# Causal attention scores from three bf16 parts of q and k, prepared by GpSimd and DMA

## What is computed

```python
q, k, v = (proj(Wq), proj(Wk), proj(Wv))
q = q * cos + _rotate_half(q) * sin      # the same for k
scores = jnp.einsum('bhqd,bhkd->bhqk', q, k) / math.sqrt(d)
scores = scores + causal
tmp_sum = jnp.sum(softmax(scores), axis=-2)
_, topk_idx = jax.lax.top_k(tmp_sum, heavy_budget)   # 25 of 256 keys per head
mask = heavy_mask | band                 # |i - j| <= 25
scores = jnp.where(mask, scores, neg)
attn = softmax(scores) @ v
x = x + attn @ Wo.T
```

## Time and profile before

| | |
|---|---|
| median of 3 runs | 2241.49 us (2239.89 to 2243.34) |
| the profiled execution | 2239.64 us, its span 2237.8 us |
| TensorE matmul busy | 2033.8 us |
| VectorE, ScalarE, GpSimd busy | 1325.7, 950.0, 230.7 us |
| granted TensorE clock, mean | 0.947 of full |

### The profile page before, as it was taken

How to read it: one execution, slowest core, us unless ns; L and a number is a source line. 1 busy time by engine, 2 the same in 40 slices (tenths; PEclk the granted TensorE clock), 3 DMA queues, 4 the chain that set the end, 5 groups by cost and what they waited for, 6 DMA issues and landing times.

```text
span 2237.8 us, 86088 instructions
## 1 busy us (share of the span) xinstructions
PE 2033.8 (91%) x34733; PEld 1748.2 (78%) x34733; DVE 1325.7 (59%) x4942; ACT 950.0 (42%) x3354; POOL 230.7 (10%) x346
## 2 busy tenths in 40 slices
PE   5889999999996889766999999998999989999999
PEld 3677677767665768666898998898998988988987
DVE  3565575575565079555666666665666656666653
ACT  1355364464453212233444444443444444444432
POOL 0011011011102100000011010110110110111012
PEclk9999999999997999865899999999999999999999
DMA  6000000000000832200000000000000000000000
GB/s 249 1 1 0 0 0 0 0 0 0 0 1 32 291 113 73 67 17 3 18 17 18 13 18 18 27 4 19 27 4 28 18 19 13 18 18 13 4 12 10
DMA packets 53629, 66.07 MB, mean 30 GB/s; under 512 B 4384, under 2 KB 45792, under 8 KB 52416
## 3 DMA queue, kind: packets, MB, share of 16 engines
q1 hardware_dynamic: 50832, 46.48, 6.2%
q0 software_dynamic: 2448, 14.68, 2.0%
HBM read 44.34 MB, written 16.81 MB: 27 GB/s over the span
## 4 chain that ended last, share of the span: by engine, by line
PE 51%; DVE 4%; issue 2%; ACT 1%; DMA 0%; DVEq 0%; POOL 0%; ACTq 0%
PE ps L1302 27%; PE ps L1256 11%; PE ps L1236 11%; PE ps L1290 2%; PE ps L1245 1%; DVE hbuf L1472 1%; DVE dh L1460 0%; DVE dh L1466 0%; DVE hbuf L1469 0%; DVE cn L1450 0%; DVE ns L1462 0%; DVE h L1470 0%; ACT nn L1369 0%; DVE s L1438 0%; DVE cn L1438 0%
## 5 line engine op out<-in xcount | busy, mean ns | idle before, releaser
L1302 PE MATMUL ps<-hbuf,whf 128*128 128x32 f16 x24480 | 659.1, 178 | 82.9 <-DVE hbuf L1472 59.9
L1302 PEld LDWEIGHTS ps<-hbuf,whf 128*128 128x128 f16 x24480 | 648.3, 97 | 106.0 <-DVE hbuf L1472 60.4
L1349 ACT ACTIVATE rz<-s,sc 128x32 f32<-128x32 f32 x512 | 164.5, 321 | 524.1 <-DVE s L1438 512.6
L1236 PE MATMUL ps<-hbuf,w1f 128*128 128x256 f16 x2304 | 294.4, 275 | 0.0
L1256 PE MATMUL ps<-hh,w2f 128*128 128x256 f16 x2304 | 294.1, 276 | 0.0
L1438 DVE TENSOR_REDUCE s<-ps 128x32 f32<-128x64 f32 x512 | 114.5, 224 | 272.7 <-PE ps L1302 259.4
L1425 POOL TENSOR_TENSOR hh<-tb,hh 128x256 f16<-128x256 f32 x192 | 132.3, 694 | 1307.2 <-ACT hh L1396 1307.2
L1236 PEld LDWEIGHTS ps<-hbuf,w1f 128*128 128x128 f16 x2304 | 224.5, 98 | 33.3 <-issue 6.0
L1256 PEld LDWEIGHTS ps<-hh,w2f 128*128 128x128 f16 x2304 | 212.0, 98 | 45.9 <-issue 19.6
L946 PE MATMUL ps<-x1T,wi 128*128 x768 | 173.7, 389 | 21.2 <-DMA wi<-in_W_ih 12.6
L946 PEld LDWEIGHTS ps<-x1T,wi 128*128 128x128 f32 x768 | 149.1, 195 | 45.4 <-issue 19.6
(11 more groups left out here) (198 smaller groups left out, 2876.3 us busy)
## 6 DMA issues: line engine op xcount, KB each, us to landing
gi_d<-stage SPq DMA_DIRECT2D x96, 128.0 KB, 1.7
gi<-gi_d SPq DMA_DIRECT2D x16, 768.0 KB, 5.5
w1f<-in_w1T POOLq DMA_DIRECT2D x4, 1408.0 KB, 9.2
xall<-in_x SPq DMA_DIRECT2D x4, 1024.0 KB, 9.0
x1T<-in_xT SPq DMA_DIRECT2D x1, 4096.0 KB, 21.7
w2f<-in_w2T POOLq DMA_DIRECT2D x2, 2048.0 KB, 11.0
out<-x1T SPq DMA_DIRECT2D x8, 512.0 KB, 3.1
wi<-in_W_ih SPq DMA_DIRECT2D x1, 3072.0 KB, 10.5
```

The source lines that it names most:

```text
L1236: last = nc.tensor.matmul(ps[:, 6 + i % 2, 0:TT], w[:, wp, e % EH, c * P:(c + 1) * P], hbuf[par][:, k, hq, :, :].rearrange("p s b -> p (s ...
L1302: last = nc.tensor.matmul(ps[:, bank, g * WIDE * 2 * B:(g + 1) * WIDE * 2 * B], whp[:, k, w, q, g * P:(g + 1) * P], h[:, k, :, :].unsqueez ...
L1349: nc.scalar.activation(rz[:, q, :, :].rearrange("p g b -> p (g b)"), s1[:, q, :, :].rearrange("p g b -> p (g b)"), ACT.Sigmoid, scale=sc[: ...
```

## The change

- TensorE no longer makes the rotation partner. SP copies the swapped halves of each 32 channels from `raw` to a tile `swp`, in 8 DMAs of 16 partitions for q and 8 for k.
- VectorE rotates in `raw` itself, in three operations each for q and k, and these stand one by one inside the second pass of the batch before, behind the work of heads 1, 2, 3, 5, 6 and 7 (`ROTATE_AT`).
- GpSimd splits the rotated float32 tile into three bf16 parts of falling size whose sum is the value (`split`: cast, subtract, cast, subtract). The four steps for q and the four for k stand ahead of the diagonals of heads 4 to 11 (`SPLIT_AT`).
- SP stores the six parts to DRAM and reads them back into `pk`, where the 32 channels of a head lie three times over on 96 partitions, each time another part (`SLOTS`). Two such stacks (`way`) hold six of the nine products of parts. A quarter of `pk` is one channel tile: 12 DMAs of 32 x 4 rows of 512 bytes. Quarter m is filled once the second pass of the batch before has done its heads.
- A score is now four bf16 products over 96 partitions: two of 128 columns, two of 256. The first pass waits at heads 0, 4, 8 and 12 for the quarters. `rot`, `kz`, `tmp` and their operations are gone.

```diff
-        rot = sb(st, "rot", [P, 2, KD, S])
-        kz = sb(st, "kz", [P, HPC, KD, S])
+        swp = sb(st, "swp", [P, KD, S])
+        parts = sb(st, "parts", [P, 2, 3, KD, S], BF16)
+        pk = sb(st, "pk", [3 * DH2, 2, 2, HPC, KD, S], BF16)
+        parts_d = nc.dram_tensor("parts_d", [2, 3, P, KD * S], BF16).ap()
...
+            @block.sync
+            def _(sp):
+                def swap(b, i):
+                    sp.wait_ge(a_raw, b * 2 + i + 1)
+                    half = DH2 // 2
+                    for to in range(0, P, half):
+                        of = to + half if to % DH2 == 0 else to - half
+                        sp.dma_start(swp[to:to + half, :, :], raw[of:of + half, i, :, :]).then_inc(d_swap, 16)
+                def store_parts(b, i):
+                    sp.wait_ge(g_part, (b * 2 + i + 1) * 4)
+                    for j in range(3):
+                        sp.dma_start(parts_d[i, j], parts[:, i, j, :, :].rearrange("p m s -> p (m s)"))\
+                            .then_inc(d_parts, 16)
+                def pack(m):
+                    for i in range(2):
+                        for way in range(2):
+                            for slot, j in enumerate(SLOTS[i][way]):
+                                of = parts_d[i, j].rearrange("(q d) n -> d q n", d=DH2)
+                                sp.dma_start(pk[slot * DH2:(slot + 1) * DH2, i, way, :, m, :],
+                                             of[:, :, m * S:(m + 1) * S]).then_inc(d_pack[m], 16)
+                def prepare(b, first):
+                    if not first:
+                        sp.wait_ge(v_rot, b * 6)
+                    swap(b, 0)
+                    sp.wait_ge(v_rot, b * 6 + 3)
+                    swap(b, 1)
+                    if not first:
+                        for m in range(KD):
+                            sp.wait_ge(d_pack[m], b * PACK)
+                    for i in range(2):
+                        store_parts(b, i)
+                    sp.wait_ge(d_parts, (b + 1) * 6 * 16)
+                    for m in range(KD):
+                        if not first:
+                            sp.wait_ge(p_s, b * 2 * NH - NH + (m + 1) * HPC + 1)
+                        pack(m)
+                for b in range(B):
+                    prepare(b, b == 0)
...
+                def split(b, i, step):
+                    if step == 0:
+                        pool.wait_ge(v_rot, b * 6 + 3 * i + 3)
+                        if b:
+                            pool.wait_ge(d_parts, b * 6 * 16)
+                    else:
+                        pool.wait_ge(g_part, (b * 2 + i) * 4 + step)
+                    x = raw[:, i, :, :]
+                    part = [parts[:, i, j, :, :] for j in range(3)]
+                    if step == 0:
+                        last = nc.gpsimd.tensor_copy(part[0], x)
+                    if step == 1:
+                        last = nc.gpsimd.tensor_tensor(x, x, part[0], ALU.subtract)
+                    if step == 2:
+                        last = nc.gpsimd.tensor_copy(part[1], x)
+                    if step == 3:
+                        last = nc.gpsimd.tensor_tensor(part[2], x, part[1], ALU.subtract)
+                    last.then_inc(g_part, 1)
+                def diagonals(b, more):
                     pool.wait_ge(v_l, b + 1)
                     for h in range(NH):
+                        if more and h in SPLIT_AT:
+                            j = SPLIT_AT.index(h)
+                            split(b + 1, j // 4, j % 4)
...
+                def batch(b, more):
                     pool.wait_ge(p_v, b + 1)
                     nc.gpsimd.tensor_copy(hb[:, :, :], hT[:, :, bass.ds(b, 1), :].rearrange("p k a s -> p k (a s)"))\
                         .then_inc(c_hb, 1)
-                    diagonals(b)
+                    diagonals(b, more)
+                for j in range(8):
+                    split(0, j // 4, j % 4)
+                for b in range(B):
+                    batch(b, b < B - 1)
...
-                    if r == 0 and h == 0:
-                        pe.wait_ge(v_rot, b * 6 + 6)
-                    if r == 0 and h < 2:
-                        pe.wait_ge(a_kz, b * 2 + h + 2)
-                    elif r == 0 and h < HPC:
-                        pe.wait_ge(v_kz, b * 2 + h - 1)
+                    if r == 0 and h % HPC == 0:
+                        pe.wait_ge(d_pack[h // HPC], (b + 1) * PACK)
...
-                    nc.tensor.matmul(ps[:, bank, 0:P], rot[:, 0, m, 0:P], kz[:, q, m, 0:P],
-                                     start=False, stop=True, skip_group_check=True)
-                    nc.tensor.matmul(ps[:, bank, P:P + S], rot[:, 0, m, P:S], kz[:, q, m, :],
-                                     start=False, stop=True, skip_group_check=True).then_inc(p_s, 1)
+                    for way in range(2):
+                        nc.tensor.matmul(ps[:, bank, 0:P], pk[:, 0, way, q, m, 0:P], pk[:, 1, way, q, m, 0:P],
+                                         start=False, stop=(way == 1), skip_group_check=True)
+                    for way in range(2):
+                        last = nc.tensor.matmul(ps[:, bank, P:P + S], pk[:, 0, way, q, m, P:S],
+                                                pk[:, 1, way, q, m, :],
+                                                start=False, stop=(way == 1), skip_group_check=True)
+                    last.then_inc(p_s, 1)
...
-                def swap(b, i):
-                    pe.wait_ge(a_raw, b * 2 + i + 1)
-                    for m in range(KD):
-                        last = nc.tensor.matmul(ps[:, 4 + 2 * i + m // 2, (m % 2) * S:(m % 2 + 1) * S],
-                                                tab[:, C_ROT:C_ROT + P], raw[:, i, m, :],
-                                                start=(m % 2 == 0), stop=True, skip_group_check=True)
-                    last.then_inc(p_rot, 1)
...
-                    if more:
-                        swap(b + 1, 0)
                     pe.wait_ge(a_o, (b + 1) * KD)
-                    if more:
-                        swap(b + 1, 1)
...
+                        if late:
+                            act.wait_ge(g_part, b * 8)
...
-                    act.wait_ge(v_rot, b * 6 + 6)
-                    for q in range(2):
-                        nc.scalar.activation(kz[:, q, :, :].rearrange("p m s -> p (m s)"),
-                                             rot[:, 1, :, :].rearrange("p m s -> p (m s)"), ACT.Copy,
-                                             scale=tab[:, C_HEAD + q:C_HEAD + q + 1]).then_inc(a_kz, 1)
...
-                def rotate(b):
-                    for i, (c, s) in enumerate(((C_COSQ, C_SINQ), (C_COSK, C_SINK))):
-                        dve.wait_ge(p_rot, b * 2 + i + 1)
-                        if i == 0:
-                            dve.wait_ge(p_s, b * 2 * NH + 1)
-                            dve.wait_ge(a_kz, b * 2 + 1)
-                        cos = tab[:, c:c + S].unsqueeze(1).broadcast_to((P, KD, S))
-                        sin = tab[:, s:s + S].unsqueeze(1).broadcast_to((P, KD, S))
-                        nc.vector.tensor_tensor(tmp[:, :, :],
-                                                ps[:, 4 + 2 * i:6 + 2 * i, :].rearrange("p a (m s) -> p (a m) s", s=S),
-                                                sin, ALU.mult).then_inc(v_rot, 1)
-                        nc.vector.tensor_tensor(rot[:, i, :, :], raw[:, i, :, :], cos, ALU.mult).then_inc(v_rot, 1)
+                def rotate(b, i, step):
+                    c, sn = ((C_COSQ, C_SINQ), (C_COSK, C_SINK))[i]
+                    cos = tab[:, c:c + S].unsqueeze(1).broadcast_to((P, KD, S))
+                    sin = tab[:, sn:sn + S].unsqueeze(1).broadcast_to((P, KD, S))
+                    if step == 0:
+                        dve.wait_ge(d_swap, (b * 2 + i + 1) * 8 * 16)
+                        nc.vector.tensor_tensor(swp[:, :, :], swp[:, :, :], sin, ALU.mult).then_inc(v_rot, 1)
+                    if step == 1:
+                        nc.vector.tensor_tensor(raw[:, i, :, :], raw[:, i, :, :], cos, ALU.mult).then_inc(v_rot, 1)
+                    if step == 2:
                         dve.wait_ge(v_rot, b * 6 + 3 * i + 2)
-                        nc.vector.tensor_tensor(rot[:, i, :, :], rot[:, i, :, :], tmp[:, :, :], ALU.add)\
+                        nc.vector.tensor_tensor(raw[:, i, :, :], raw[:, i, :, :], swp[:, :, :], ALU.add)\
                             .then_inc(v_rot, 1)
-                        dve.wait_ge(v_rot, b * 6 + 3 * i + 3)
-                    for q in range(2, HPC):
-                        nc.vector.tensor_scalar(kz[:, q, :, :], rot[:, 1, :, :], tab[:, C_HEAD + q:C_HEAD + q + 1],
-                                                None, ALU.mult).then_inc(v_kz, 1)
...
-                    if more:
-                        rotate(b + 1)
+                        if more and h in ROTATE_AT:
+                            j = ROTATE_AT.index(h)
```

(25 more changed lines are left out.)

11 lines of the change are left out of this document (3 added, 8 removed).

## The result

The changed kernel takes **2347.6 us** (median of 4 runs, 2336.8 to 2353.5) against 2242.1 (4 runs, 2239.9 to 2243.3): 1.047 times as long, 95% interval 1.042 to 1.051. The profiled execution took 2343.6 us, its span is 2341.7. The time lies inside the range on record, but 46 us above the predicted 2302 and 2 us under the range's upper end of 2350; two of the four runs are above that end. The change cost 105 us where 62 were forecast.

A forecast was written before the change was run, and what follows sets the result against it. Three engines stand together near the first pass's bound; GpSimd's splits would hold up the second. Seven longer periods +32, contention +14, clock +10, start +16, last batch -10: +62 on 2239.6 gives 2302 us, range 2262 to 2350.

The forecast's parts named there:

- First pass: First score to end of the `lcol` copy: ScalarE sets the pace at 0.95 us per head, 36.0 instead of 38.6.
- Contention: Second pass: `En` delayed by shared access with GpSimd, 2 us per batch between bounds 0 and 6, +14 in all.
- the chain on record: Second pass: rotations, GpSimd's splits, diagonals and maxima step by step, last `En` at 39.7 us after `lcol` instead of 26.0.
- Tail: Last `En` to the next batch's first score: 10.4 us instead of 15.4, the wait for rotation and `kz` gone.
- Clock: TensorE's lower granted clock, charged to second pass and before the output product: 1.5 us per batch (0 to 3.5), +10.
- Last batch: Both passes without rotation or split: first gains 4.6 us, second takes 22.7 instead of 28.2; -10.
- Start: Batch 0, swaps, rotation, split and packs without cover: first quarter packed at 89.6 against 74.4; +16 us.
- The third rival: Second attention: contention and clock at their upper bounds, period 95.6 us, 2351 us in all; chance 0.20.

The follow-up runs named there:

- Small splits: Changed kernel with the four split operations covering 32 elements instead of 1024 from batch 1 on, at their places: 2301.4 us.
- late ones: Changed kernel with the eight split steps before the diagonals of heads 8 to 15 instead of 4 to 11: 2317.4 us.
- the scores alone: Kernel before the change, with scores as bf16 products of the new shape on a constant tile, rotation and `kz` as before: 2213.2 us.
- the run with more TensorE work: Changed kernel with eight extra mask products, result overwritten, before the second-pass scores of heads 4 to 11: 2342.2 us.
- one way: Changed kernel with each score multiplying only the first of its two packed stacks, 384 columns instead of 768: 2362.8 us.
- adds first: Kernel before the change, with VectorE's two `kz` operations behind its four `x1T` adds instead of ahead of them: 2224.1 us.

## Why the prediction was right, and where it was short

*Right: direction, bound, place.* GpSimd's split, in one queue with the diagonals, sets the second pass: TensorE waits 105.2 us for them. Small splits (-46) and late ones (-30) confirm it. They also show how near the next bound stands: with the waits for diagonals at 2.8 us, VectorE's own chain still took 39.7. The subtract is 2.12 us (taken as 2.2 between 1.04 and 2.8). The single steps of the chain held while nothing contended: q rotated 9.7 (10.1), maxima of head 4 12.6 (12.6), of head 5 15.2 (15.4). TensorE waited for packs in batch 0 only. The gain of the scores was small because three engines stand together at the first pass's bound, as the scores alone show.

*First pass: 37.1, not 36.0.* ScalarE kept its pace (14 heads in 13.5 us, 0.96 each), but value products started 14.4 us after the first score, not 13.2: a set of light-sum products (L581) stood ahead of score 15, waited 0.66 us for VectorE and took 0.86, which my count left out.

*Contention: the term that failed.* I took 2 us per batch of bounds 0 and 6, arguing that VectorE has slack where GpSimd is the bound. It has none behind a blocked `En`. Against the chain on record, k was rotated at 24.5 instead of 22.7, 1.8 of it from the `En` pair at 433.70; head 11's maxima began at 34.9 instead of 32.5, another pair behind the second subtract of k; and heads 12 to 15 took 1.8 more again, 1.2 of it one pair behind a diagonal and the copy of `hb`, the rest a pitch of 1.28, not 1.19 us. That pitch is no contention: the scores-only run has it too. In VectorE's rows of the changed kernel's batch 3:

```profile
448.50 1.71 DVE L795 TENSOR_SCALAR En<-E,rl 128x128 f32<-128x128 f32 x1
450.13 0.72 DVE L797 TENSOR_SCALAR En<-E,rl 128x256 f32<-128x256 f32 x1
...
453.35 0.71 DVE L795 TENSOR_SCALAR En<-E,rl 128x128 f32<-128x128 f32 x1
453.98 1.12 DVE L797 TENSOR_SCALAR En<-E,rl 128x256 f32<-128x256 f32 x1
```

Against an undisturbed pair (0.55 us from the start of the one to the end of the other) the three lose 1.8, 1.8 and 1.2 us, not all of it on the chain (the pairs of heads 4 and 8 lose 1.2 each as well, beside the second casts); the pass came out at 43.9 in this batch and 44.3 on the mean, against 39.7 + 2. So contention cost some 4 us per batch, 25 to 30 us in all instead of +14, and well towards the bound of 6, though by another pair of instructions: the `En` operations, not the rotation products (their mean of 1.22 is unchanged here, since GpSimd had no split to do beside them). Only with splits later did a rotation product meet one.

*Tail: 11.6, not 10.4*, with a gap of 0.89 us before the next batch (under 1 was forecast). It goes with the clock: the tail took 10.7 us in the three batches that had 1.00, and 12.0 to 12.4 in the four that had 0.86.

*Clock.* Of the 1.5 charged per batch the tail shows 0.9 (11.6 on the mean for 10.7 at full clock). The first passes of batches 1 to 6 had 1.00, and the run with more TensorE work shows that the second pass pays little. So the place was another than I charged, the size somewhat smaller. That a low clock can reach the first pass is shown by one way (+2.2 at 0.83).

*Last batch: -6.6, not -10.* Its first pass took 30.4 at a clock of 0.95, not 28.9: not all of the clock's loss was curable. Its second pass took 24.6, not 22.7, and here the clock is not the cause: with scores of the same cost it takes 24.2 us in the scores-only run, at a clock of 1.00 in six batches and of 0.91 in the last. My 15 steps of 1.25 were too short for VectorE.

*Start: +22, not +16.* No step was missing, but each swap took longer than my 4.4: the first 8.0 us from its first issue to VectorE's product, the second 6.7 from the end of q's rotation. SP's issues of the swaps in the changed kernel (ns of one, min/median/max, then landing):

```profile
L422 SPq DMA_DIRECT2D swp<-raw x128: 507/589/1657, 57.0 to 711.7; - x128
...
DMA to landing us min/median/max: 2.2/2.3/3.4
```

Eight issues of 0.59 and a landing of 2.3 are 7.0; the 4.4 came from the stores of `gi_d`. The two swaps add 5.9 us, the stores and the first quarter's packs (issues of 0.43) 2.7 more, and q stood in `raw` 1.3 earlier. A price taken from transfers of another shape should have had a range of its own. The same excess is the swap wait of the small splits. Batch 0's first pass also took 42.8, not the 36.6 I allowed: TensorE waited 2.7 us in it for later quarters, and had a clock of 0.82, where the first passes behind it had 1.00 and took 37.1.

*The sum.* Against the terms on record a period came out 4.2 us longer: first pass +1.9 (0.7 of it from batch 0), second pass with contention +2.6, tail +1.2, less the 1.5 charged for the clock. Seven times that is 29; the start adds 6 and the last batch 3.4, which makes 39 of the 42 us by which the profiled execution missed 2302. Some 2 more lie behind the second attention, and the median is 4 above that execution. The range held all this by 2 us only.

The third rival (2351, chance 0.20) came nearer than the forecast. Its mechanism, the exclusive lock, is what the runs show. That its number is so near is in part luck: it charged 6 us per batch for contention and 3.5 for the clock, where some 4 and 1 are seen, and these made up for the first pass and the start, which its sum had too short as the forecast's did.

Not tried: all diagonals of a batch ahead of the splits (it needs a buffer for each), swaps over two queues, adds first together with bf16 scores.

## What to carry to other kernels

A part of a product's work moved to an idle engine is not free if that engine feeds the chain: look at what else stands in its queue and at which element-wise instructions it will meet, and charge each meeting with the whole rest of the longer one. Before paying for a cheaper product, run the product alone on constant data: here the cheaper scores by themselves were worth 1.3%. And look at short pauses of TensorE by their clock: a reordering of two operations that cut one from 2.7 to 1.6 us brought 0.8%, about half of it in first passes and in the last batch, where the low clock behind the pause went too.

## What the runs showed of the hardware that I had not expected

- An `En` of 0.29 us beside a GpSimd subtract took 1.70, and 14 of 14 ended 0.08 to 0.09 us after the subtract; a two-input product of 1.22 beside one took 2.46, ending 1.08 after it; a diagonal of 0.61 beside that product took 1.32. The wait goes both ways.
- Fewer products on TensorE made the kernel slower by 15 us, through a lower granted clock (0.83 for 1.00 in most first passes).
- A pause of TensorE of 2.69 us was followed by a granted clock of 0.54 over the next 3 us (5 of 21 pauses of 2.5 to 2.8 us were not followed by a low clock), one of 1.4 to 1.6 us by 1.00 in each of seven batches.
- An issue on SP's queue took 0.33 (`gi_d`), 0.43 (stores of parts, packs) or 0.59 us (swaps) at the median, and single ones up to 1.66 (swaps) and 1.75 (packs).
